# First attention: values and sums in four bursts a step instead of six

## The chip, the cores and the metric

The kernel runs on one core of one Trainium2 chip. The metric is the device time in microseconds of one execution of the whole program. Times are in microseconds (us). The engines are named PE (TensorE, matmuls), PEld (its weight loads, which overlap), DVE (VectorE), ACT (ScalarE), POOL (GpSimd) and SP (SyncE, which issues most DMAs).

## What is computed

Two transformer layers over x of 2 x 1024 x 512. The change lies in the attention of the first one, which is multi-head attention with latent keys and values, rotary parts and a causal mask:

```python
q = _rmsnorm(x @ wq_a.T, q_a_ln_w) @ wq_b.T              # 32 heads of 64 + 64 (rotary)
ckv, k_pe = ckv_kpe[..., :KVR], ckv_kpe[..., KVR:]       # latent of 32, rotary key of 64
kv = _rmsnorm(ckv, kv_a_ln_w) @ wkv_b.T                  # keys 64 and values 128 a head
scores = jnp.einsum('bqhd,bkhd->bhqk', q_full, k_full) * softmax_scale
scores = jnp.where(causal[None, None], scores, jnp.finfo(scores.dtype).min)
attn = jax.nn.softmax(scores, axis=-1)
out = jnp.einsum('bhqk,bkhd->bqhd', attn, v).reshape(B, S, H * VD)
return out @ wo.T
```

Layer norms with modulation, a feed-forward part with routed low-rank experts, a second attention with shared keys and a second feed-forward part surround it.

## The kernel before

`attention0` handles 4 heads of one batch in a **step** t; there are STEPS0 = 16 steps. Scores are computed transposed, keys on the partitions and 512 queries along the row. A step has 12 **quads** n, one for each pair of a query half qc and a key tile kt of 128 that the causal mask leaves: quads 0 to 3 are the first half (kt 0 to 3), quads 4 to 11 the second (kt 0 to 7). On the diagonal (quads 0 to 3 and 8 to 11) a quad covers 512, 384, 256 and 128 queries; the last two of these pack two and four heads in one score unit, so the quads have 4, 4, 2, 1, 4, 4, 4, 4, 4, 4, 2, 1 units, 38 a step.

For each unit PE makes three matmuls into one of two PSUM banks (`score`, L985 to L989, with a fourth, L987, for the mask on the diagonal), and ACT writes the exponential (`exps`, L886) into one of 16 slots of `at_prob`. Unit x waits until the exponential of unit x - 2 is done, and a slot until the quad that used it has been consumed (`pv_done`). Between the units PE issues **pieces**: query projections of step t + 2 (`project_q`, L1037) and matmuls for row maxima (`maximum`, L1000), which DVE reduces (L916, L921); these use a ring of 4 banks. `quad_work` lists the pieces of a quad.

`values(g, part)` (L1022) takes the probabilities of a quad through 32-column matmuls, for each of the 4 heads into its own 32 partitions: part 0 with the latents `l_cn` into the bank `at_op`, part 1 with ones into `at_dp`. In the trace each of these matmuls is two records, so two quads are x16. For quads 4 to 7 part 1 is left out: POOL adds their probabilities beforehand (`presum` 1, 2, 3, L816), and PE sums the result in `early_sums` (L1031). Before the change a burst of two quads, 10-11, 0-1, 2-3, 4-5, 6-7 and 8-9, stands behind the scores of each odd quad 1, 3, 5, 7, 9 and 11; MID_AT says how many maxima stand between its two parts.

The order of the other engines is fixed too, each in its own program. ACT: the exponentials of a quad; behind quad 2 the copy out of the second query half of the step before, behind quad 6 that of the first half (`copy_out`, L856 and L857), for which `values` of quads 0 and 4 wait (`u_copied`); behind quads 7 and 10 the conversion of a half of the projected queries of step t + 2 (`queries_hi`, L873), which waits for POOL's rotation (`rot_done`). POOL in steps 1 to 13: presum 1, rotate half 0 (L791, L792), low parts of half 0 (L802, waits for `queries_hi`), presums 2 and 3, `normalise` (L820), rotate half 1, low parts of half 1. PE turns the maxima of the step's second half with a transpose (`turn_maxima`, L1009) ahead of quad 2 (in the first step ahead of quad 4); it waits for DVE's last maximum and its join (L926). The result goes through ACT (L863) and a DMA into the queries that quad 4 needs.

Of the kernel before, what the change touches and what calls it, by code (L numbers as in the profile page):

```python
# [600 lines left out]
QUADS = UNITS // G  # L601
STEPS0 = B * NG
# [5 lines left out]
FIRST_HALF = 4 * G  # L608
OWN_AT = [{0: 8, 1: 8, 2: 8, 3: 8}, {0: 3, 1: 3}]
MAX_AT = [{6: 8, 7: 8, 8: 7, 9: 7, 10: 6, 11: 6}, {2: 4, 3: 4, 4: 5, 5: 5, 6: 4, 7: 6, 8: 4, 9: 4, 10: 3, 11: 3}]  # L610
MID_AT = {3: 2, 5: 3, 7: 3, 9: 2, 11: 2}
PROJ_AT = [{7: (0,), 8: (1, 2), 9: (3,), 10: (4, 5)}, {4: (0,), 5: (1,), 6: (2,), 7: (3,), 8: (4,), 9: (5,)}]
PROJ_FIRST = {1: (0, 1, 2), 2: (3, 4, 5)}
TURN_A, TURN_B = 9, (4, 2)
# [11 lines left out]
EARLY = [n for n, (qc, kt) in enumerate(QK) if kt < 4 * qc]  # L626
# [44 lines left out]
def attention0(nc, k, s, opened, o_dram, sums, recips, next_loads):  # L671

    with ExitStack() as ctx:
# [46 lines left out]
        with nc.Block() as block:  # L720
# [247 lines left out]
            def _(pe):  # L968
# [58 lines left out]
                def early_sums(t):  # L1027
                    pe.wait_ge(s["pre_done"], 3 * G * (t + 1))
                    pe.wait_ge(s["u_copied"], 2 * (2 * t + 1))
                    for j in range(G):  # L1030
                        mm = nc.tensor.matmul(dp[LAT * j:LAT * (j + 1), :], k.ones[:], pre[:, j, :], start=True, stop=False)  # L1031
                    mm.then_inc(s["pre_used"], 1)

                def project_q(t, u):
                    hf, part = u // 3, u % 3
                    freed(pe, "queries", t, u)
                    nc.tensor.matmul(bank("queries", t, u)[:], k.wq[:, t % NG, part, :], k.qa_t[:, t // NG, HALF * hf:HALF * (hf + 1)],  # L1037
                                     start=True, stop=True).then_inc(s["pj_ready"], 1)
# [7 lines left out]
                for g in range(STEPS0 * QUADS):  # L1046
                    t, n = divmod(g, QUADS)
                    for which in turns(t, n):
                        turn_maxima(*which)
                    if n == 0:  # L1050
                        moved(pe, lo_in, t)
                        pe.wait_ge(m_in[t % 2], 16 * (t // 2 + 1))
                    if n == 4:
                        pe.wait_ge(m_late[t % 2], 16 * (t // 2 + 1))
                    pieces = quad_work(t, n)
                    between = max(len(pieces) - MID_AT.get(n, 0), 0)
                    cut = [round(between * i / UNITS_OF[n]) for i in range(UNITS_OF[n] + 1)]
                    for i in range(UNITS_OF[n]):
                        score(t, n, i)
                        for kind, to, u in pieces[cut[i]:cut[i + 1]]:  # L1060
                            if kind == "queries":
                                project_q(to, u)
                            if kind == "max":
                                maximum(to, u)
                    if g % 2 and g >= 3:
                        for part in range(2):
                            for kind, to, u in pieces[between:] if part == 1 else ():
                                maximum(to, u)
                            if part == 1 and (g - 3) % QUADS in EARLY:
                                if (g - 2) % QUADS == EARLY[-1]:  # L1070
                                    early_sums((g - 3) // QUADS)
                                continue
                            values(g - 3, part)
                            values(g - 2, part)
                for part in range(2):
                    values(STEPS0 * QUADS - 2, part)
                    values(STEPS0 * QUADS - 1, part)


RG = 64  # L1080
# [1089 lines left out]
```

## Time and profile before

| | |
|---|---|
| median of 3 runs | 2156.2 us (2155.67 to 2158.36) |
| the profiled execution | 2149.3 us |
| its span, first to last instruction | 2147.5 us |
| PE busy | 1968.2 us (92%) |
| DVE, ACT, POOL busy | 1174.7, 903.5, 524.4 us |
| mean granted TensorE clock | 0.945 |

The first attention runs from about 145 us to 1117 us of the span. Matmuls are pipelined and their ends are modelled, so in the timeline the distance from one start to the next says more than a duration.

### The profile page before, as it was taken

The numbers are of one execution on the slowest core, as the hardware profiler recorded it, in microseconds if no ns is written. First come the engines' busy times: TensorE is split into PE (matmuls) and PEld (weight loads), VectorE is DVE, ScalarE is ACT, GpSimd is POOL, SyncE is SP. The second block draws the span as 40 slices with busy tenths as digits, with TensorE's granted clock in tenths as the row PEclk, the third lists the DMA queues.
The fourth block names the chain that finished last, engine by engine and source line by source line (L and its number), as shares of the span: only waits on it lengthen the run. The fifth ranks groups of instructions, "written<-read, shape, count | busy, mean of one in ns | idle before, by whom it ended". The sixth has DMA issues, their size and how long they took to land. (4 is left out here: it accounts for less than half of the span.)

```text
span 2147.5 us, 34578 instructions
## 1 busy us (share of the span) xinstructions
PE 1968.2 (92%) x12776; PEld 1173.9 (55%) x12776; DVE 1174.7 (55%) x2557; ACT 903.5 (42%) x1909; POOL 524.4 (24%) x408
## 2 busy tenths in 40 slices
PE   5859999999999999999977899997999999999698
PEld 4535666666666666666643454554444444444277
DVE  3546655555555555555402455446676776675078
ACT  3413344444444444444430122221666656666344
POOL 0014235555434443555330000000000000000143
PEclk9869999999999999999998999995999999999599
DMA  9752233222233323322235221144132132220121
GB/s 310 258 155 60 61 80 81 70 58 57 69 81 80 80 71 80 80 67 59 56 107 189 66 67 48 58 113 125 22 53 47 33 53 45 35 38 18 33 87 59
DMA packets 113594, 172.21 MB, mean 80 GB/s; under 512 B 26186, under 2 KB 46826, under 8 KB 113298
## 3 DMA queue, kind: packets, MB, share of 16 engines
q1 hardware_dynamic: 112402, 169.75, 29.9%
q8 instruction: 101, 1.65, 0.3%
q14 instruction: 67, 0.55, 0.1%
q10 hardware_dynamic: 1024, 0.26, 0.1%
HBM read 84.32 MB, written 29.38 MB: 53 GB/s over the span
## 5 line engine op out<-in xcount | busy, mean ns | idle before, releaser
L886 ACT ACTIVATE at_prob<-at_scp 128x512 f32<-128x512 f32 (+1 forms) x608 | 349.7, 576 | 512.2 <-PE at_scp L989 511.0
L1659 ACT ACTIVATE as_prob<-as_scp 128x512 f32<-128x512 f32 (+2 forms) x640 | 309.0, 563 | 200.3 <-PE as_scp L1769 148.9
L921 DVE CUSTOM_DVE_ANT_0 at_junk<-at_mxp,causal 128x128 f32<-128x128 f32 (+3 forms) x512 | 243.4, 488 | 188.6 <-PE at_mxp L1000 183.9
L1709 DVE TENSOR_REDUCE as_mxd<-as_mxp 128x2 f32<-128x256 f32 (+3 forms) x256 | 202.6, 820 | 98.3 <-PE as_mxp L1788 96.1
L916 DVE TENSOR_REDUCE at_mxf<-at_mxp 128x1 f32<-128x512 f32 x256 | 175.9, 687 | 141.3 <-PE at_mxp L1000 137.4
L1694 POOL TENSOR_TENSOR l_att_t<-l_att_t,as_spread 64x1024 f32<-64x1024 f32 x16 | 37.9, 2367 | 863.2 <-DMA as_spread<-l_recips 863.2
L1707 DVE TENSOR_REDUCE as_mxf<-as_mxp 128x2 f32<-128x1024 f32 x128 | 151.0, 1221 | 52.8 <-PE as_mxp L1783 52.6
L816 POOL TENSOR_TENSOR at_pre<-at_prob 128x512 f32<-128x512 f32 x64 | 80.1, 1281 | 407.2 <-ACT at_prob L886 407.2
L816 POOL TENSOR_TENSOR at_pre<-at_pre,at_prob 128x512 f32<-128x512 f32 x128 | 160.3, 1282 | 3.6 <-ACT at_prob L886 1.2
L1807 PE MATMUL as_op<-as_prob,l_vn 128*32 128x512 f32 (+3 forms) x1536 | 160.4, 540 | 0.0
L1022 PE MATMUL at_op<-at_prob,l_cn 128*32 128x512 f32 (+3 forms) x1536 | 143.7, 491 | 4.0 <-ACT at_u_sb L857 4.0
L985 PE MATMUL at_scp<-hd_early_q,l_khi 97*128 97x512 f32 (+1 forms) x304 | 137.2, 451 | 10.8 <-DMA hd_late_q<-at_slo 8.3
L985 PE MATMUL at_scp<-at_qhi,l_khi 97*128 97x512 f32 (+1 forms) x304 | 138.8, 456 | 0.8 <-ACT at_prob L886 0.5
L1000 PE MATMUL at_mxp<-l_khi,hd_early_q 96*128 96x512 f32 (+2 forms) x384 | 125.2, 379 | 10.9 <-DMA hd_early_q<-at_shi 9.3
L1000 PE MATMUL at_mxp<-l_khi,at_qhi 96*128 96x512 f32 (+2 forms) x384 | 122.5, 367 | 0.5 <-DVE at_mxf L916 0.2
L988 PE MATMUL at_scp<-hd_late_q,l_khi 96*128 96x512 f32 (+1 forms) x304 | 117.2, 386 | 0.0
L989 PE MATMUL at_scp<-hd_early_q,l_klo 96*128 96x512 f32 (+1 forms) x304 | 116.8, 384 | 0.0
L988 PE MATMUL at_scp<-at_qlo,l_khi 96*128 96x512 f32 (+1 forms) x304 | 116.8, 384 | 0.0
L989 PE MATMUL at_scp<-at_qhi,l_klo 96*128 96x512 f32 (+1 forms) x304 | 116.3, 383 | 0.0
L1766 PE MATMUL as_scp<-as_q,l_keys 49*128 49x512 f32 (+2 forms) x320 | 108.1, 463 | 7.8 <-ACT as_prob L1659 6.5
L1783 PE MATMUL as_mxp<-l_keys,hd_early_q 48*128 48x512 f32 (+2 forms) x384 | 97.7, 488 | 19.2 <-DVE as_mxf L1707 7.3
L1766 PE MATMUL as_scp<-hd_early_q,l_keys 49*128 49x512 f32 (+2 forms) x320 | 103.7, 446 | 5.7 <-ACT as_prob L1659 4.3
(248 smaller groups left out, 3480.5 us busy)
## 6 DMA issues: line engine op xcount, KB each, us to landing
hd_late_q<-at_slo SPq DMA_DIRECT2D x96, 128.0 KB, 2.4
at_qhi<-at_shi SPq DMA_DIRECT2D x96, 128.0 KB, 2.4
at_qlo<-at_slo SPq DMA_DIRECT2D x96, 128.0 KB, 2.5
hd_early_q<-at_shi SPq DMA_DIRECT2D x84, 128.0 KB, 2.5
at_spread<-l_recips SPq DMA_DIRECT2D x64, 128.0 KB, 2.7
l_o<-at_u_sb SPq DMA_DIRECT2D x16, 512.0 KB, 3.3
hd_early<-in_wmod SPq DMA_DIRECT2D x7, 1024.0 KB, 7.4
hd_late<-l_o SPq DMA_DIRECT2D x12, 512.0 KB, 4.1
```

The source lines that it names most:

```text
L816: nc.gpsimd.tensor_tensor(pre[:, j, :], other, prob[:, (x + j) % RING0, :], ALU.add).then_inc(s["pre_done"], 1)
L886: nc.scalar.activation(prob[:, x % RING0, c0:HALF], scp[x % BANKS0][:, c0:HALF], ACT.Exp).then_inc(s["exp_done"], 1)
L916: nc.vector.reduce_max(mxf[:, j, qt - 4:qt - 3], tile[:], AX_X).then_inc(s["mx_done"], 1)
L921: nc.vector.tensor_tensor_reduce(out=junk[:, u % 2, 0:w], in0=tile[:, 0:w], in1=k.causal[:, HALF - w:HALF], scale=1.0, scalar=LOWEST, op0= ...
L985: nc.tensor.matmul(out, k.khi[0:KR + 1, b, ks], q_cols(qhi[t % 2][0:KR + 1]), start=True, stop=False)
L988: nc.tensor.matmul(out, k.khi[0:KR, b, ks], q_cols(qlo[t % 2][0:KR]), start=False, stop=False)
L989: nc.tensor.matmul(out, k.klo[0:KR, b, ks], q_cols(qhi[t % 2][0:KR]), start=False, stop=True).then_inc(s["sc_ready"], 1)
L1000: nc.tensor.matmul(bank("max", t, u)[:, 0:w], qhi[t % 2][0:KR, qt // 4, j, qt % 4 * P:(qt % 4 + 1) * P], k.khi[0:KR, t // NG, k0:k0 + w], ...
L1659: nc.scalar.activation(prob[:, x % RING1, cols], scp[x % BANKS1][:, cols], ACT.Exp).then_inc(s["exp_done"], 1)
L1709: nc.vector.reduce_max(mxd[:, t % 2, :, i, qt:qt + 1], tile[:, :, 0:(qt % 4 + 1) * P], AX_X).then_inc(s["mx_done"], 1)
L1766: mm = nc.tensor.matmul(out, k.keys[rows, t // NG, kt * P:(kt + 1) * P], queries, start=True, stop=not diagonal)
L1807: mm = nc.tensor.matmul(op[2 * HD * j:2 * HD * (j + 1), c0:HALF], k.vn[:, t // NG, kt, :], prob[:, (x + j % UNITS1_OF[n]) % RING1, p0:p0 + ...
```

## The change

The values and sums are issued in bursts listed by the new table BURSTS0: behind the scores of quad 0 those of quads 8 to 11 of the step before, behind quad 4 those of quads 0 to 3, behind quad 6 the values of 4 and 5, behind quad 8 those of 6 and 7. In a burst all values come first, then the maxima that MID_AT keeps (3, 3 and 2 at quads 0, 4 and 8), then the sums; the early sums stand with the sums of quads 8 to 11. The other engines' programs are as they were. In the changed kernel the line numbers from 612 on are 1 higher (L985 is L986, L1022 is L1023, L1031 is L1032), and behind the new function `sums` 12 higher (L1037 is L1049).

```diff
--- before.py
+++ after.py
@@ -608,7 +608,8 @@
 FIRST_HALF = 4 * G
 OWN_AT = [{0: 8, 1: 8, 2: 8, 3: 8}, {0: 3, 1: 3}]
 MAX_AT = [{6: 8, 7: 8, 8: 7, 9: 7, 10: 6, 11: 6}, {2: 4, 3: 4, 4: 5, 5: 5, 6: 4, 7: 6, 8: 4, 9: 4, 10: 3, 11: 3}]
-MID_AT = {3: 2, 5: 3, 7: 3, 9: 2, 11: 2}
+MID_AT = {0: 3, 4: 3, 8: 2}
+BURSTS0 = {0: (-4, -3, -2, -1), 4: (0, 1, 2, 3), 6: (4, 5), 8: (6, 7)}
 PROJ_AT = [{7: (0,), 8: (1, 2), 9: (3,), 10: (4, 5)}, {4: (0,), 5: (1,), 6: (2,), 7: (3,), 8: (4,), 9: (5,)}]
 PROJ_FIRST = {1: (0, 1, 2), 2: (3, 4, 5)}
 TURN_A, TURN_B = 9, (4, 2)
@@ -1031,6 +1032,17 @@
                         mm = nc.tensor.matmul(dp[LAT * j:LAT * (j + 1), :], k.ones[:], pre[:, j, :], start=True, stop=False)
                     mm.then_inc(s["pre_used"], 1)
 
+                def sums(burst, between):
+                    for q in burst:
+                        values(q, 0)
+                    for kind, to, u in between:
+                        maximum(to, u)
+                    for q in burst:
+                        if q % QUADS == EARLY[-1] + 1:
+                            early_sums(q // QUADS)
+                        if q % QUADS not in EARLY:
+                            values(q, 1)
+
                 def project_q(t, u):
                     hf, part = u // 3, u % 3
                     freed(pe, "queries", t, u)
@@ -1053,7 +1065,8 @@
                     if n == 4:
                         pe.wait_ge(m_late[t % 2], 16 * (t // 2 + 1))
                     pieces = quad_work(t, n)
-                    between = max(len(pieces) - MID_AT.get(n, 0), 0)
+                    burst = [QUADS * t + i for i in BURSTS0.get(n, ()) if QUADS * t + i >= 0]
+                    between = max(len(pieces) - MID_AT.get(n, 0), 0) if burst else len(pieces)
                     cut = [round(between * i / UNITS_OF[n]) for i in range(UNITS_OF[n] + 1)]
                     for i in range(UNITS_OF[n]):
                         score(t, n, i)
@@ -1062,19 +1075,8 @@
                                 project_q(to, u)
                             if kind == "max":
                                 maximum(to, u)
-                    if g % 2 and g >= 3:
-                        for part in range(2):
-                            for kind, to, u in pieces[between:] if part == 1 else ():
-                                maximum(to, u)
-                            if part == 1 and (g - 3) % QUADS in EARLY:
-                                if (g - 2) % QUADS == EARLY[-1]:
-                                    early_sums((g - 3) // QUADS)
-                                continue
-                            values(g - 3, part)
-                            values(g - 2, part)
-                for part in range(2):
-                    values(STEPS0 * QUADS - 2, part)
-                    values(STEPS0 * QUADS - 1, part)
+                    sums(burst, pieces[between:])
+                sums(range(STEPS0 * QUADS - 4, STEPS0 * QUADS), ())
 
 
 RG = 64
```

PE at the end of a step, from the one unit of quad 11 on to the first unit of the next step. Before:

```order
L985 MATMUL at_scp<-hd_early_q,l_khi 128x512
L987 MATMUL at_scp<-after_r,ident_r 128x512
L988 MATMUL at_scp<-hd_late_q,l_khi 128x512
L989 MATMUL at_scp<-hd_early_q,l_klo 128x512
L1000 MATMUL at_mxp<-l_khi,at_qhi 128x512
L1022 MATMUL at_op<-at_prob,l_cn 32x512 x4
L1022 MATMUL at_op<-at_prob,l_cn 32x384 x4
L1000 MATMUL at_mxp<-l_khi,at_qhi 128x512
L1000 MATMUL at_mxp<-l_khi,at_qhi 128x256
L1022 MATMUL at_dp<-at_prob,ones 32x512 x4
L1022 MATMUL at_dp<-at_prob,ones 32x384 x4
L985 MATMUL at_scp<-at_qhi,l_khi 128x512
```

Now, from the same unit on:

```order
L986 MATMUL at_scp<-hd_early_q,l_khi 128x512
L988 MATMUL at_scp<-after_r,ident_r 128x512
L989 MATMUL at_scp<-hd_late_q,l_khi 128x512
L990 MATMUL at_scp<-hd_early_q,l_klo 128x512
L1001 MATMUL at_mxp<-l_khi,at_qhi 128x512 x2
L1001 MATMUL at_mxp<-l_khi,at_qhi 128x256
L986 MATMUL at_scp<-at_qhi,l_khi 128x512
L988 MATMUL at_scp<-after_r,ident_r 128x256
L989 MATMUL at_scp<-at_qlo,l_khi 128x512
L990 MATMUL at_scp<-at_qhi,l_klo 128x512
L986 MATMUL at_scp<-at_qhi,l_khi 128x512
L988 MATMUL at_scp<-after_r,ident_r 128x256
```

The values (`at_op`) and sums (`at_dp`) of quads 8 and 9 are no longer between the two steps; two units of the next step stand behind each other.

PE at the end of quad 6 (its last unit, and the first of quad 7). Before:

```order
L985 MATMUL at_scp<-hd_early_q,l_khi 128x512
L988 MATMUL at_scp<-hd_late_q,l_khi 128x512
L989 MATMUL at_scp<-hd_early_q,l_klo 128x512
L1000 MATMUL at_mxp<-l_khi,at_qhi 128x384
L985 MATMUL at_scp<-hd_early_q,l_khi 128x512
L988 MATMUL at_scp<-hd_late_q,l_khi 128x512
L989 MATMUL at_scp<-hd_early_q,l_klo 128x512
L1037 MATMUL at_mxp<-l_qa_t,l_wq 128x512
```

Now:

```order
L986 MATMUL at_scp<-hd_early_q,l_khi 128x512
L989 MATMUL at_scp<-hd_late_q,l_khi 128x512
L990 MATMUL at_scp<-hd_early_q,l_klo 128x512
L1001 MATMUL at_mxp<-l_khi,at_qhi 128x384
L1023 MATMUL at_op<-at_prob,l_cn 32x512 x8
L986 MATMUL at_scp<-hd_early_q,l_khi 128x512
L989 MATMUL at_scp<-hd_late_q,l_khi 128x512
L990 MATMUL at_scp<-hd_early_q,l_klo 128x512
```

The values of quads 4 and 5 now stand directly behind the last unit of quad 6.

PE at the end of quad 1 with the turn ahead of quad 2. Before:

```order
L989 MATMUL at_scp<-at_qhi,l_klo 128x384
L1000 MATMUL at_mxp<-l_khi,at_qhi 128x512
L1022 MATMUL at_op<-at_prob,l_cn 32x256 x4
L1022 MATMUL at_op<-at_prob,l_cn 32x128 x4
L1022 MATMUL at_dp<-at_prob,ones 32x256 x4
L1022 MATMUL at_dp<-at_prob,ones 32x128 x4
L1009 MATMUL at_mxp<-ident,at_mxd 16x128
L985 MATMUL at_scp<-at_qhi,l_khi 128x512
```

Now:

```order
L990 MATMUL at_scp<-at_qhi,l_klo 128x384
L1001 MATMUL at_mxp<-l_khi,at_qhi 128x512
L1010 MATMUL at_mxp<-ident,at_mxd 16x128
L986 MATMUL at_scp<-at_qhi,l_khi 128x512
L988 MATMUL at_scp<-after_r,ident_r 128x2x128
```

The burst of quads 10 and 11 no longer stands between the last maximum and the transpose.

## Rows read from the trace of the kernel before

**Rows 1.** Busy time by stretch; columns as in the first line.
```profile
core 0: us, PE busy (x) PEld busy (x) DVE busy (x) ACT busy (x) POOL busy (x), PEclk, DMA share, GB/s
600.00:620.00 20.00, 19.76 (x137) 12.68 (x138) 10.38 (x38) 8.85 (x17) 0.00 (x0) 1.00 0.53 130
620.00:640.00 20.00, 20.00 (x119) 13.45 (x111) 14.19 (x35) 9.64 (x19) 14.76 (x12) 1.00 0.11 29
```

**Rows 2.** Waits of PE and of ACT, 200 to 1100 us; total, times, longest.
```profile
PE at_dp L1031 <- POOL at_pre L816: 5.9, 13, 0.5
PE at_op L1022 <- ACT at_u_sb L857: 4.0, 15, 0.7
...
ACT at_shi L873 <- POOL at_tm L792: 10.3, 13, 0.8
```

**Rows 3.** Timeline of PE, quad 7's last unit and burst; start, duration.
```profile
630.01 0.40 PE L985 MATMUL at_scp<-at_qhi,l_khi 97*128 97x512 f32 x1
...
630.71 0.40 PE L1000 MATMUL at_mxp<-l_khi,hd_early_q 96*128 96x512 f32 x1
631.04 1.92 PE L1022 MATMUL at_op<-at_prob,l_cn 128*32 128x512 f32 x16
632.89 0.74 PE L1000 MATMUL at_mxp<-l_khi,hd_early_q 96*128 96x256 f32 x3
```

**Rows 4.** Timeline of PE, the early sums behind quad 9.
```profile
645.45 1.07 PE L1031 MATMUL at_dp<-at_pre,ones 128*32 128x512 f32 x8 [0.47 <-POOL at_pre L816]
646.45 0.50 PE L985 MATMUL at_scp<-at_qhi,l_khi 97*128 97x512 f32 x1
```

**Rows 5.** Timelines of PE and of DVE at the turn ahead of quad 2.
```profile
601.30 0.39 PE L1000 MATMUL at_mxp<-l_khi,at_qhi 96*128 96x512 f32 x1
601.62 0.86 PE L1022 MATMUL at_op<-at_prob,l_cn 128*32 128x256 f32 x16
...
603.06 0.28 PE L1009 MATMUL at_mxp<-ident,at_mxd 128*16 128x128 f32 x1
...
601.91 0.69 DVE L921 CUSTOM_DVE_ANT_0 at_junk<-at_mxp,causal 128x512 f32<-128x512 f32 x1 [1.04 <-PE at_mxp L1000]
...
602.64 0.17 DVE L926 TENSOR_TENSOR at_mxd<-at_mxd,at_mxf 128x16 f32<-128x16 f32 x1
```

**Rows 6.** Timelines of PE and of ACT at the two copies.
```profile
607.03 1.71 PE L1022 MATMUL at_op<-at_prob,l_cn 128*32 128x512 f32 x16 [0.24 <-ACT at_u_sb L857]
...
626.60 0.39 PE L985 MATMUL at_scp<-at_qhi,l_khi 97*128 97x512 f32 x1
...
606.28 0.60 ACT L857 ACTIVATE at_u_sb<-at_op 128x512 f32<-128x512 f32 x1
...
627.66 0.60 ACT L857 ACTIVATE at_u_sb<-at_op 128x512 f32<-128x512 f32 x1
```

**Rows 7.** Timelines of POOL, ACT and PE from quad 7 to the next step.
```profile
632.74 2.52 POOL L802 TENSOR_TENSOR at_slo<-at_tm,at_shi 128x512 fp32r<-128x512 f32 x2 [4.83 <-ACT at_shi L873]
635.22 10.17 POOL L816 TENSOR_TENSOR at_pre<-at_pre,at_prob 128x512 f32<-128x512 f32 x8
645.36 2.38 POOL L820 TENSOR_TENSOR at_u_sb<-at_u_sb,at_spread 128x1024 f32<-128x1024 f32 x1
647.71 1.29 POOL L791 TENSOR_TENSOR at_tm<-at_tm 128x512 f32<-128x512 f32 x1
648.97 1.28 POOL L792 TENSOR_TENSOR at_tm<-at_tm 128x512 f32<-128x512 f32 x1
...
630.97 0.60 ACT L886 ACTIVATE at_prob<-at_scp 128x512 f32<-128x512 f32 x1 [0.34 <-PE at_scp L989]
...
650.28 1.15 ACT L873 ACTIVATE at_shi<-at_tm 128x512 fp32r<-128x512 f32 x2 [0.82 <-POOL at_tm L792]
651.34 0.58 ACT L886 ACTIVATE at_prob<-at_scp 128x512 f32<-128x512 f32 x1
...
655.05 0.39 PE L985 MATMUL at_scp<-hd_early_q,l_khi 97*128 97x512 f32 x1
```

**Rows 8.** Busy time by stretch in the opening; columns as in rows 1.
```profile
103.40:106.00 2.60, 0.20 (x2) 0.00 (x0) 2.50 (x10) 0.60 (x1) 0.00 (x0) 1.00 1.01 353
...
108.00:109.00 1.00, 1.00 (x2) 0.50 (x2) 0.59 (x2) 0.00 (x0) 0.00 (x0) 0.50 1.11 326
```

## The prediction

> **What bounds the kernel now.** I read the busy times in stretches of 20 us first: inside the first attention TensorE (PE) is busy 19.76 and 20.00 us of 20 at a granted clock of 1.00, which is its upper level, 2.4 GHz [rows 1]. So time there is PE time: whatever is taken from PE shortens a step, whatever makes PE wait lengthens it. Next the waits by engine [rows 2]: in 900 us PE waits for another engine only in two regular places, 5.9 us in 13 times for POOL's pre-sums (0.45 us each) and 4.0 us in 15 times for ACT's copy of the output bank (0.27 us each). The third row is the one that matters most below: ACT waits 10.3 us in 13 times (0.79 us each) for POOL's rotated queries, and nothing comes of it, because PE does not need ACT at that moment. Then the timeline of one step, at the places where bursts are taken away or put in.
>
> **Part 1: fewer blocks of 32-column matmuls.** A block is a run of values, sums or early sums between full-width matmuls. The 16 instructions of 512 columns at 631.04 are followed 1.85 us later [rows 3]; the 8 at 645.45 by a score 1.00 us later [rows 4]. The difference, 0.85 us, is the work of 8, so a block has 0.15 us that doesn't grow with it. The maximum before the first of them starts at 630.71 and would be followed after 0.23 us, but the block starts at 631.04: 0.10 us on entering; on leaving I take the same 0.10. A block costs 0.35 us beside its work. Before there are 10 blocks in a step (quads 10-11 as one; two each for 0-1, 2-3, 8-9; one for 4-5; two for 6-7 with the early sums), after it 6 (two for 8-11 with the early sums, two for 0-3, one each for 4-5 and 6-7). Gain: 4 x 0.35 = 1.4 us a step.
> The Trainium skill weighs this less: TensorEngine Tiling (Array Packing), Key Properties, says that a change of tiling mode drains TensorE, and TensorE: Matmul & The Clock Gate, "What happens when you issue a matmul", puts a drain at about 128 cycles, 0.05 us at 2.4 GHz. Two changes a block would by that estimate be 0.1 us, the gain 0.4 us a step, and the end 16 us later than the sum below. The rows measure the block whole, so I stay with 0.35.
>
> **Part 2: waits that go.** The values of quad 0 now come after the scores of quad 4, so the copy at quad 2 is long done: 0.27 us gained. The early sums go from quad 9 to the next step's quad 0: POOL's pre-sums are then done, 0.45 us gained. Maxima put between scores of quads 5 and 9 instead of inside a block save about 0.1 us, but the three taken from quad 0 leave four scores in a row with nothing between, where each waits for the exponential two before it: 0.15 us lost. Together with part 1: 2.1 us gained a step.
>
> **Part 3: the turn at quad 2 loses its cover.** The transpose of the maxima (L1009) waits for DVE's last maximum of the step and its join. Its last matmul starts at 601.30; DVE works from 601.91 to 602.81; the burst of quads 10-11 filled the time until 603.06 [rows 5]. After the change nothing stands between: PE would be ready at 601.53 and gets the join at about 602.98. Loss 1.45 us, and the scores of quad 2 queue behind it. Bounds: 1.3 us (join seen at once) to 1.55 us.
>
> **Part 4: the output bank at quad 6.** Values of quad 4 start a new accumulation in the bank that ACT copies out after the exponentials of quad 6. They move from behind quad 7 to right behind quad 6. PE ends quad 6 at 626.60, or 626.70 with the entry of a block; ACT's second copy starts at 627.66 and takes 0.60 us; in another place PE started 0.15 us after such a copy ended (606.28 + 0.60 to 607.03) [rows 6]. So PE starts at 628.41: 1.7 us lost a step, all of PE's queue behind it. Bounds 1.5 to 1.9.
> Parts 1 to 4 leave 3.3 - 2.1 = 1.2 us a step lost, about 18 us in 15 steps; in the first step, where DVE is late, the burst at quad 3 covered a wait and moves behind it, some 4 us. **Local sum: +22 us.**
>
> **Part 5: POOL's chain at the end of a step.** This is the large one. POOL runs in program order: low parts of one query half (they wait for ACT's conversion behind the exponentials of quad 7), pre-sums 2 and 3, normalise, rotate the other half. In the rows: 632.74, 635.22, 645.36, 647.71, 648.97, end 650.25 [rows 7]. It can't start before ACT's last exponential of quad 7, which starts at 630.97, so its end hangs 18.7 us behind that one's end at 631.57. ACT, also in order, has the conversion of that second half between the exponentials of quads 10 and 11: 650.28, and only at 651.34 the exponential of quad 11, which ends at 651.92 [rows 7]. PE's second score of the next step needs its bank. Today PE comes there at 655.05, 3.0 us later [rows 7]: that is the cover.
> Now the time that PE takes from the last score unit of quad 7 (starts 630.01 [rows 3]) to that second score, 25.04 us, shrinks. Out of it go: the block of quads 4-5, 2 x 0.85 + 0.35 = 2.05 us; two of the maxima of quad 7, which now stand before the unit, 0.35 us; the early sums with their wait, 0.85 + 0.35 + 0.45 = 1.65 us; the values and the sums of quads 8-9, each 8 instructions of 512 columns (0.85 us), 8 of 384 (0.64 us) and a block's 0.35 us, together 3.7 us; the maximum between the first two scores of quad 0, 0.23 us. What is left is 17.1 us. POOL's chain isn't any shorter: exponential of quad 11 ends 21.9 us behind the start of that unit, plus 0.15 us for PE to see it, 22.05. **PE waits 5.0 us** at the second score of a step, behind it in its queue all else; SP's loads of the next queries wait for the same conversion, and keep their distance to their use. It holds for steps 1 to 13, those with queries to project and this chain, as the 13 waits of ACT today [rows 2]: 13 x 5.0 = 65 us. Bounds of one wait: 4.0 us if I have missed a microsecond of work in between, 5.5 us.
>
> **Part 6: the clock.** No row of the first attention's steady state shows PE at less than full clock. Nearest rows: before 106 PE stood idle for 2.4 of 2.6 us, and at 108 the granted clock is 0.50, that is 1.2 GHz [rows 8]. After 5 us of standing I expect a stretch at the lower level. How long isn't known; from nothing (it falls into the wait itself) to some 2.5 us lost each. I take 1.5: 13 x 1.5 = 20 us.
>
> **Sum.** 22 + 65 + 20 = 107 us on the profiled execution, 2149.3 + 107 = 2256. The median of the runs is 6.9 us above the profiled execution, so **2263 us** as a median.
>
> **Rivals.**
> (A) The forecast, all three terms: 2263, from 2240 to 2285. Chance 0.58.
> (B) The chain binds, the clock stays up: 2156 + 22 + 65 = 2243; with waits of 4.0 us and local losses of 0.6 us, 2156 + 10 + 52 = 2218. For it: only PE waits of several us lower the clock, and part of the lower stretch falls into the wait. Chance 0.17.
> (C) The clock also falls after the waits of 1.45 and 1.7 us in parts 3 and 4: 32 places at up to 1.7 us, 2263 + 54 = 2317. The steady state has few gaps elsewhere, which speaks against it. Chance 0.08.
> (D) POOL's chain doesn't bind, because its early part moves up with PE or because ACT isn't waited for: local losses alone, 2156 + 22 = 2178. Against it: today POOL waits 4.83 us for ACT before the chain starts [rows 7], so nothing of it can move up. Chance 0.09.
> (E) Faster: the block savings remain and the waits don't come. Its place is quad 6 and quad 2, its price is 2.1 us x 16 = 34 us, 2122. It decides if PE's time in front of the two waits is longer by 1.5 us than its instructions show, as it would be if DVE and ACT finished ahead. The rows 5 and 6 show both in the middle of their work when PE is ready. Chance 0.05.
> (F) Gains and losses cancel: POOL's chain not binding and one of parts 3 and 4 half as dear: within 0.2% of before. Chance 0.03.
> That the change does not do what it says is excluded: the instruction order shows four bursts.
>
> **How the numbers follow.** Likeliest is A, so 2263. Range: A whole and B whole, with part of C, 2216 to 2300; out are D, E, F and most of C, 0.2. A measurement can tell about 0.2% here. Slower by more than 0.2% is A to D, 0.92; within 0.2% 0.03; faster 0.05.
>
> **What the profile of the changed kernel would show.** PE waiting for ACT's exponential at a score (L985's successor) 13 times, about 5 us each; ACT waiting for POOL's rotation 13 times, about 4.9 us (today's 0.8 and the 4.05 us that part 5 takes out ahead of it); PE waiting for ACT's output copy 16 times at 1.7 us, and for DVE's join 15 times at 1.4; the waits for the pre-sums gone. Granted clock below 1.00 in the stretch behind each start of a step from 260 us on. POOL's own chain as long as before, 18.7 us from the last exponential of quad 7. Wrong would be: a step of 61 us (then D), or PE's waits at the right places but the clock at 1.00 (B).

## The result, and the profile after

The changed kernel takes 2279.6 us (median of 4 runs, 2275.6 to 2280.1), the kernel before 2157.0 us: ratio 1.0566, 95% interval 1.0549 to 1.0582. The forecast was 2263 in a range of 2216 to 2300. The profiled execution has a span of 2278.3 us against 2147.5: 130.8 us more.

The lines below are numbered differently by a few: the score L985 is now L986, the maximum L1000 is L1001, the turn L1009 is L1010, values and sums L1022 are L1023, ACT's exponential L886 is L887, its conversion of queries L873 is L874.

The busy times and the granted clock in 40 slices, from the page of the changed kernel:

```profile
PE 1998.5 (88%) x12776; PEld 1208.8 (53%) x12776; DVE 1164.0 (51%) x2557; ACT 904.2 (40%) x1909; POOL 523.7 (23%) x408
PEclk8868999999999999999999799999699999999689
```

The same 12776 matmuls; PE is busy 30 us longer (1968.2 before) and idle for the other 100. The waits from 200 to 1230 us (total, times, longest), which answer to [rows 2]:

```profile
PE at_scp L986 <- ACT at_prob L887: 61.9, 14, 4.7
PE at_op L1023 <- ACT at_u_sb L858: 26.2, 16, 1.8
PE at_mxp L1010 <- DVE at_mxd L927: 17.7, 15, 1.2
...
ACT at_shi L874 <- POOL at_tm L793: 63.3, 13, 4.9
```

PE's wait for POOL's pre-sums is gone, ACT's wait for POOL's rotated queries has grown from 10.3 to 63.3 us in the same 13 places, and PE now waits for ACT behind it. In one stretch of a step (its bounds, its length, then busy time of PE, PEld, DVE, ACT and POOL, granted clock, DMA share, GB/s), for [rows 1]:

```profile
640.00:660.00 20.00, 15.28 (x74) 11.21 (x74) 9.97 (x25) 6.96 (x14) 16.95 (x13) 0.88 0.13 30
```

**The start of a step.** PE's timeline (start, duration, line and operation, in brackets the idle time before it and what ended it), for PE's row of [rows 7]:

```profile
651.19 0.39 PE L990 MATMUL at_scp<-at_qhi,l_klo 96*128 96x512 f32 x1
656.31 0.80 PE L986 MATMUL at_scp<-at_qhi,l_khi 97*128 97x512 f32 x1 [4.72 <-ACT at_prob L887]
...
657.11 0.63 PE L989 MATMUL at_scp<-at_qlo,l_khi 96*128 96x512 f32 x1
```

A matmul of 512 columns that took 0.39 us before the wait takes 0.63 behind it. POOL in the same step:

```profile
637.13 2.53 POOL L803 TENSOR_TENSOR at_slo<-at_tm,at_shi 128x512 fp32r<-128x512 f32 x2 [6.67 <-ACT at_shi L874]
639.61 10.20 POOL L817 TENSOR_TENSOR at_pre<-at_pre,at_prob 128x512 f32<-128x512 f32 x8
649.77 2.37 POOL L821 TENSOR_TENSOR at_u_sb<-at_u_sb,at_spread 128x1024 f32<-128x1024 f32 x1
...
653.34 1.25 POOL L793 TENSOR_TENSOR at_tm<-at_tm 128x512 f32<-128x512 f32 x1
```

And ACT, from the last exponential of quad 7 to the one that PE waits for:

```profile
635.35 0.60 ACT L887 ACTIVATE at_prob<-at_scp 128x512 f32<-128x512 f32 x1 [0.21 <-PE at_scp L990]
...
654.62 1.15 ACT L874 ACTIVATE at_shi<-at_tm 128x512 fp32r<-128x512 f32 x2 [4.60 <-POOL at_tm L793]
655.68 1.06 ACT L887 ACTIVATE at_prob<-at_scp 128x512 f32<-128x512 f32 x2
```

The last exponential of quad 7 ends at 635.95, POOL's rotation at 654.6: 18.6 us. The conversion starts at once, the exponential of quad 11 a microsecond later, and PE when that is through. One stretch behind it, in the columns of the window above:

```profile
656.30:661.90 5.60, 5.59 (x16) 3.65 (x20) 0.00 (x0) 2.23 (x4) 2.11 (x2) 0.50 0.77 174
```

The clock is at 1.2 GHz in the 5.6 us behind the wait, in which PE isn't idle: 2.8 us lost. From 662 on it is back at 1.00.

**The two smaller waits**, at quad 6 and at the turn of quad 2, for [rows 6] and [rows 5]:

```profile
628.66 1.92 PE L1023 MATMUL at_op<-at_prob,l_cn 128*32 128x512 f32 x16 [1.64 <-ACT at_u_sb L858]
...
670.80 0.40 PE L1001 MATMUL at_mxp<-l_khi,at_qhi 96*128 96x512 f32 x1
...
672.15 0.18 DVE L927 TENSOR_TENSOR at_mxd<-at_mxd,at_mxf 128x16 f32<-128x16 f32 x1
672.39 0.28 PE L1010 MATMUL at_mxp<-ident,at_mxd 128*16 128x128 f32 x1 [1.19 <-DVE at_mxd L927]
```

The number in brackets counts from the modelled end of the matmul before, the prediction counted from start to start. In its way of counting the transpose is 672.39 - 670.80 - 0.23 = 1.36 us late. The burst at quad 6 follows a maximum that starts at 626.68; with 0.17 us for that one and 0.10 for the entry of a block it is 1.71 us late. The score at the start of a step is 656.31 - 651.19 - 0.23 = 4.89 us late.

**Where the 130.8 us are.** The turn at quad 9 is a mark in every step. It starts like this before (first, seventh, eighth and fifteenth step):

```profile
216.37 0.27 PE L1009 MATMUL at_mxp<-ident,at_mxd 128*16 128x128 f32 x1
578.79 0.27 PE L1009 MATMUL at_mxp<-ident,at_mxd 128*16 128x128 f32 x1
638.46 0.27 PE L1009 MATMUL at_mxp<-ident,at_mxd 128*16 128x128 f32 x1
1052.41 0.27 PE L1009 MATMUL at_mxp<-ident,at_mxd 128*16 128x128 f32 x1
```

and after:

```profile
229.96 0.27 PE L1010 MATMUL at_mxp<-ident,at_mxd 128*16 128x128 f32 x1
574.27 0.27 PE L1010 MATMUL at_mxp<-ident,at_mxd 128*16 128x128 f32 x1
642.52 0.27 PE L1010 MATMUL at_mxp<-ident,at_mxd 128*16 128x128 f32 x1
1184.24 0.27 PE L1010 MATMUL at_mxp<-ident,at_mxd 128*16 128x128 f32 x1
```

(574.27 is the mark of the sixth step, 642.52 that of the seventh.) A step in the middle takes 68.25 us instead of 59.67: +8.6, twelve times. The first mark is 13.6 us late. The second step's is another 7.0 us late (70.98 us for 64.02), the fifteenth's another 8.0 (63.86 for 55.90), and behind it 1.0 comes back: 13.6 + 7.0 + 12 x 8.6 + 8.0 - 1.0 = 130.8.

Not all of the 13.6 belongs to the change. One maximum in the opening, ahead of every moved burst, is late already. Before, then after:

```profile
177.13 0.50 PE L1000 MATMUL at_mxp<-l_khi,hd_early_q 96*128 96x512 f32 x1 [0.63 <-DVE at_pre L946]
```

```profile
181.05 0.50 PE L1001 MATMUL at_mxp<-l_khi,hd_early_q 96*128 96x512 f32 x1 [0.63 <-DVE at_pre L947]
```

These 3.9 us are mostly scatter of the opening. In the profiles of the kernels below that share before's opening that row starts from 177.1 to 180.8, in those with the changed kernel's from 179.3 to 183.8; before's is the earliest of all, in an execution that was 6.9 us faster than its median. Some 2 us between the two groups' means may belong to the change. Between this row and the first mark lie 39.2 us before and 48.9 after, 9.7 more, but that isn't the change's alone either. The kernel of experiment 9 (early_only) has the program of before up to this mark, and takes 43.2 us:

```profile
180.19 0.50 PE L1000 MATMUL at_mxp<-l_khi,hd_early_q 96*128 96x512 f32 x1 [0.63 <-DVE at_pre L946]
...
223.36 0.27 PE L1009 MATMUL at_mxp<-ident,at_mxd 128*16 128x128 f32 x1
```

Its granted clock is at 0.50 in two stretches there (from 198 to 202, for one), where the profile of before stays at 1.00. The five profiled kernels that have the changed kernel's program up to the mark take 46.8 to 50.5 us. So the change costs between 4 and 11 us in this stretch, about 7 by the means.

### The profile page after: what moved, and what is told of

Read it like the earlier page. It is cut to its first block and busy times, and to the rows that moved or that the text cites. A ratio compares the mean times of both kernels' runs of the same rounds, so it can differ in the third digit from the quotient of the medians.

```text
span 2278.3 us, 34578 instructions
## 1 busy us (share of the span) xinstructions
PE 1998.5 (88%) x12776; PEld 1208.8 (53%) x12776; DVE 1164.0 (51%) x2557; ACT 904.2 (40%) x1909; POOL 523.7 (23%) x408
## 5 line engine op out<-in xcount | busy, mean ns | idle before, releaser
L887 ACT ACTIVATE at_prob<-at_scp 128x512 f32<-128x512 f32 (+1 forms) x608 | 348.1, 575 | 557.3 <-PE at_scp L990 556.1
L986 PE MATMUL at_scp<-hd_early_q,l_khi 97*128 97x512 f32 (+1 forms) x304 | 140.7, 463 | 44.0 <-ACT at_prob L887 33.1
L986 PE MATMUL at_scp<-at_qhi,l_khi 97*128 97x512 f32 (+1 forms) x304 | 139.8, 460 | 29.1 <-ACT at_prob L887 28.8
L1023 PE MATMUL at_op<-at_prob,l_cn 128*32 128x512 f32 (+3 forms) x1536 | 142.2, 503 | 26.2 <-ACT at_u_sb L858 26.2
L1001 PE MATMUL at_mxp<-l_khi,hd_early_q 96*128 96x512 f32 (+2 forms) x384 | 124.3, 390 | 10.2 <-DMA hd_early_q<-at_shi 9.0
L989 PE MATMUL at_scp<-hd_late_q,l_khi 96*128 96x512 f32 (+1 forms) x304 | 124.0, 408 | 0.0
L990 PE MATMUL at_scp<-hd_early_q,l_klo 96*128 96x512 f32 (+1 forms) x304 | 123.4, 406 | 0.0
L1001 PE MATMUL at_mxp<-l_khi,at_qhi 96*128 96x512 f32 (+2 forms) x384 | 121.1, 377 | 2.4 <-DVE at_tm L947 2.2
L989 PE MATMUL at_scp<-at_qlo,l_khi 96*128 96x512 f32 (+1 forms) x304 | 121.4, 399 | 0.0
L990 PE MATMUL at_scp<-at_qhi,l_klo 96*128 96x512 f32 (+1 forms) x304 | 121.0, 398 | 0.0
L988 PE MATMUL at_scp<-after_r,ident_r 128*128 128x256 f32 (+1 forms) x352 | 109.5, 311 | 0.0
```

What stands on the lines that cost most here:

```text
L887: nc.scalar.activation(prob[:, x % RING0, c0:HALF], scp[x % BANKS0][:, c0:HALF], ACT.Exp).then_inc(s["exp_done"], 1)
L986: nc.tensor.matmul(out, k.khi[0:KR + 1, b, ks], q_cols(qhi[t % 2][0:KR + 1]), start=True, stop=False)
L989: nc.tensor.matmul(out, k.khi[0:KR, b, ks], q_cols(qlo[t % 2][0:KR]), start=False, stop=False)
L990: nc.tensor.matmul(out, k.klo[0:KR, b, ks], q_cols(qhi[t % 2][0:KR]), start=False, stop=True).then_inc(s["sc_ready"], 1)
L1001: nc.tensor.matmul(bank("max", t, u)[:, 0:w], qhi[t % 2][0:KR, qt // 4, j, qt % 4 * P:(qt % 4 + 1) * P], k.khi[0:KR, t // NG, k0:k0 + w], ...
```

## Experiments

Each ratio is to the kernel before, run beside it on the same chip. "Step" is the distance of two marks in the middle of the attention.

**1. The conversion leaves the chain (hi_late).** The changed kernel, ACT's conversion of the second query half moved behind the next step's exponentials of quad 0.

```diff
                         exps(t, n)
+                        if n == 0 and t >= 1 and t + 1 < STEPS0:
+                            queries_hi(t + 1, 1)
                         for which in queries_ready(t, n):
-                            queries_hi(*which)
+                            if which[1] == 0 or which[0] == 1:
+                                queries_hi(*which)
```

> The changed kernel with one move on ACT: the conversion of the second query half stands behind the exponentials of the next step's quad 0 instead of between those of quads 10 and 11. Theory (POOL's chain holds up the exponential of quad 11, and the clock falls behind that wait): PE's 62 us of waiting for exponentials go, the granted clock stays at 1.00, a step goes from 68.3 to about 60.8 us, the whole from 2279.6 to about 2183 us. Rival (the clock falls because of the long bursts or the waits at quads 2 and 6): the waits go, but the low clock stays, about 2215 us. Rival (the chain is a bystander): over 2250 us.

2191.3 us, ratio 1.0157 (1.0140 to 1.0173): 88 of the change's 123 us are gone with this one edit. PE's waits from 200 to 1230 us:

```profile
PE at_op L1026 <- ACT at_u_sb L858: 26.2, 16, 1.8
PE at_mxp L1013 <- DVE at_mxd L930: 17.8, 15, 1.2
...
PE at_scp L989 <- ACT at_prob L887: 0.3, 1, 0.3
```

The two small waits stand as they were, the 61.9 us are 0.3. The shortest steps take 60.93 us: the change without its chain costs 1.25 us a step (the forecast had 1.2). Other steps take up to 62.86. In one of these the clock falls behind the wait at quad 6, and the 16 values take 3.50 us instead of 1.92:

```profile
655.58 3.50 PE L1026 MATMUL at_op<-at_prob,l_cn 128*32 128x512 f32 x16 [1.64 <-ACT at_u_sb L858]
```

Over 60.93 the twelve middle steps have 5.7 us together, most of the 8 between expectation and result. What the full step of the changed kernel has on top, 68.25 - 60.93 = 7.3 us, is the wait of 4.7 and 2.6 for the clock (4.9 and 2.4 if the wait is counted from start to start).

**2. A shorter chain (norm_late).** The changed kernel, POOL rotates before it normalises, which takes 2.4 us out of the chain.

```diff
+                    if t + 2 < STEPS0:
+                        rotate(t + 2, 1)
                     if t >= 1:
                         normalise(t - 1)
                     if t + 2 < STEPS0:
-                        rotate(t + 2, 1)
                         low_parts(t + 2, 1)
```

> The changed kernel with POOL's rotation of the second query half ahead of the normalise step, so that the chain is shorter by the 2.4 us of normalise. Theory: PE's wait at the second score of a step falls from 4.7 to about 2.4 us, 13 x 2.4 = 31 us less. If the clock falls only behind a wait of several us, another 13 x 2.4 us go with it, 2217 us in all; if it falls as long as before, 2248 us. If the chain isn't the cause, no change (2279.6 us).

2239.8 us, 1.0395 (1.0370 to 1.0421), between the two expectations. The wait is shorter by about what left the chain, and the stretch at the lower clock by half: 3.4 us instead of 6.8 in most steps. PE's timeline, then the window behind it:

```profile
639.22 0.49 PE L987 MATMUL at_scp<-at_qhi,l_khi 97*128 97x512 f32 x1 [2.45 <-ACT at_prob L888]
...
639.67 0.39 PE L990 MATMUL at_scp<-at_qlo,l_khi 96*128 96x512 f32 x1
```

```profile
640.50:643.90 3.40, 3.40 (x16) 1.72 (x18) 0.00 (x0) 1.71 (x3) 1.79 (x2) 0.50 0.89 200
```

After 2.45 us of standing PE works 1.3 us at 2.4 GHz and then 3.4 us at 1.2. Most steps take 64.97 us; 60.93 + 2.45 (the wait) + 3.4/2 is 65.08. I had expected either no stretch or the whole one.

**3. The copy (copy_early).** The changed kernel, the copy of the output bank behind the exponentials of quad 5 (`if n == 6:` becomes `if n == 5:` before `copy_out(t, 0)`).

> The changed kernel with ACT's copy of the first query half's output behind the exponentials of quad 5 instead of quad 6. Theory: PE's 26.2 us of waiting for that copy go (16 x 1.64 us), and since this place lies ahead of POOL's chain nothing takes them back: 2253 us. Rival (the chain's wait grows by what is saved): no change, 2279.6 us.

2255.0 us, 1.0456 (1.0439 to 1.0473). The wait at quad 6 is no longer in the list, the one at the start of a step is untouched:

```profile
PE at_scp L986 <- ACT at_prob L887: 63.1, 16, 4.8
```

26.2 us of waits gone, 24.5 us of time: a wait on PE's path counts nearly in full. It doesn't feed the chain either, because POOL's chain hangs on quad 7, which comes later and moves along.

**4. The price of a block (no_mid).** The kernel before with `MID_AT = {}`: the maxima stay with the scores, and four blocks of 32-column matmuls in a step are no longer cut in two.

> The kernel before with no maxima kept inside the bursts (MID_AT empty): they stand between the scores, and values and sums of a burst are one block. 10 blocks of 32-column matmuls a step become 6 with all other places as they were; behind quad 7 the number of blocks stays 1. Theory (a block costs 0.35 us beside its work, as taken in the prediction): 16 x 4 x 0.35 = 22 us less, 2135 us. By the drain of the Trainium skill (0.1 us a block): 6 us less, 2151 us. If DVE then makes PE wait, less than that.

2141.0 us, 0.9931 (0.9916 to 0.9946). The step is 58.65, 1.03 us shorter. PE's waits:

```profile
PE at_dp L1031 <- POOL at_pre L816: 13.5, 13, 1.1
PE at_op L1022 <- ACT at_u_sb L857: 0.6, 1, 0.6
```

The wait for the pre-sums has grown from 0.45 to 1.04 us, since PE is there sooner and POOL is not; the copy's 0.27 has gone. Four blocks are therefore worth 1.03 + 0.59 - 0.27 = 1.35 us, 0.34 each. The 6 us missing against the 2135 expected are mostly this longer wait, 13 x 0.59 = 8 us.

**5. Quads 8 and 9 apart (split89).** The changed kernel, with the values of quads 8-9 and the early sums behind quad 11, and only 10-11 in the next step's quad 0.

```diff
-BURSTS0 = {0: (-4, -3, -2, -1), 4: (0, 1, 2, 3), 6: (4, 5), 8: (6, 7)}
+BURSTS0 = {0: (-2, -1), 4: (0, 1, 2, 3), 6: (4, 5), 8: (6, 7), 11: (8, 9)}
```

> The changed kernel with the burst of quads 8 to 11 taken apart again: quads 8 and 9 with the early sums behind quad 11, quads 10 and 11 behind the next quad 0 (5 bursts). This undoes one part of the change. Theory: 3.7 us of values and sums and 1.2 us of early sums stand again in front of the second score of a step, so PE's wait of 4.7 us there goes and with it the low clock; one block more costs 0.35 us. A step of 68.3 becomes about 61.3 us, the whole 2279.6 - 13 x 7.0 = 2189 us. Rival (the chain hangs on the early sums' place in some other way, or the clock on the long burst of quads 0 to 3): over 2230 us.

2212.3 us, 1.0258 (1.0243 to 1.0273). PE and ACT (from each engine's waits):

```profile
PE at_scp L986 <- ACT at_prob L887: 8.4, 14, 0.6
...
ACT at_shi L874 <- POOL at_tm L793: 64.1, 13, 5.0
```

ACT waits for POOL as long as in the changed kernel, and PE hardly notices: the burst is the cover. ACT's own wait is no sign of harm. The miss of 23 us: the quicker steps take 62.1 us and not 61.3, since 0.6 us of PE's wait is left; five of the middle steps take 63.7 to 64 us, with 3.4 us at the lower clock behind the wait at quad 6; and the second step is 2.5 us longer than in the changed kernel.

**6. The first step (first3).** The changed kernel, its burst of quads 0-3 behind quad 3 in the first step only (with three maxima kept inside it).

> The changed kernel, in the first step alone the burst of quads 0 to 3 stands behind quad 3 instead of quad 4, and so in front of the turn as before the change. Theory: the first step's loss (the start of its quad 9 went from 216.4 to 230.0 us, 13.6 us) is PE's uncovered wait for DVE's last maximum and the low clock that follows it: 8 to 10 us less, 2270 us. Rival (it is the second burst order itself): no change, 2279.6 us.

2275.2 us, 1.0552 (1.0534 to 1.0569), 4 us below the changed kernel; the intervals overlap, so the time alone doesn't settle it. The mark of the first step does, 4.8 us earlier than the changed kernel's 229.96:

```profile
225.20 0.27 PE L1011 MATMUL at_mxp<-ident,at_mxd 128*16 128x128 f32 x1
```

The burst covers the turn again, and the clock is low for a shorter stretch. The 4.8 us are about half of the 8 to 10 expected. Both kernels still pay the copy's wait there.

**7. The turn (own42).** The changed kernel, maxima of quads 0 and 1 divided 4 and 2 instead of 3 and 3 (`OWN_AT = [..., {0: 4, 1: 2}]`), so that DVE has less left at the turn.

> The changed kernel with the step's own maxima as 4 and 2 on quads 0 and 1 instead of 3 and 3, so that the last one stands ahead of quad 1's last unit. Theory: PE's wait at the turn, 1.18 us a step, is covered by a unit of 0.65 us: 15 x 0.65 = 10 us less, 2270 us. With the chain's wait in the same step untouched nothing takes it back. Rival (the wait moves to the exponentials of quad 1): no change.

2281.3 us, 1.0572 (1.0556 to 1.0588): the same as the changed kernel. The wait is shorter, from 17.7 to 7.8 us, and yet nothing is gained. PE's timeline at quad 6 and the window of that burst show why:

```profile
492.36 3.62 PE L1023 MATMUL at_op<-at_prob,l_cn 128*32 128x512 f32 x16 [1.64 <-ACT at_u_sb L858]
```

```profile
492.40:495.80 3.40, 3.40 (x16) 0.67 (x16) 0.00 (x0) 0.00 (x0) 1.75 (x2) 0.51 0.18 48
```

The wait of 1.64 us is the one that the changed kernel has in each step without harm. Here five steps, every other one from 352 to 902 us, have 3.4 us at 1.2 GHz behind it, 1.7 us lost in each, which takes back most of the 10 us that the turn gives. So it is rival C's mechanism, in a kernel for which I hadn't named it. Why it strikes here and not there is open.

**8. All four repairs (all4).** The changed kernel with the edits of hi_late, copy_early, own42 and first3 together.

> The changed kernel with four moves at once: the second conversion behind the next quad 0, the copy behind quad 5, own maxima 4 and 2, the first step's burst behind quad 3. Theory: the four bursts then keep their gain without the waits: a step of 60.9 (conversion moved) less 1.64 (copy) less 0.65 (turn) is 58.6 us against 59.7 before, the whole 2156 - 15 x 1.1 = 2140 us. Rival (the savings of the bursts are smaller than taken): 2156 or more.

2165.1 us, 1.0039 (1.0024 to 1.0053). The best steps take 59.24, others 59.8 to 61.7. PE has new waits, for loads that follow the late conversion:

```profile
PE at_mxp L1005 <- DMA at_qhi<-at_shi: 5.6, 7, 1.6
PE at_mxp L1005 <- DMA hd_early_q<-at_shi: 5.3, 7, 1.7
```

Moving the conversion back opens the one wait and exposes the next thing in line: SP's loads of the queries. The three slowest middle steps (61.7 to 61.9 us) are the ones where such a wait lasts 1.4 to 1.6 us and 3.4 us at 1.2 GHz follow (at 321, 741 and 802 us); in the other slower steps the granted clock stays at 1.00. The result is 25 us above what I expected.

**9. Only the early sums (early_only).** The kernel before, early sums with the sums of quads 8-9 behind quad 11.

> The kernel before with another part of the change alone: the early sums stand with the sums of quads 8 and 9, behind quad 11, instead of behind quad 9. Theory: PE's wait for POOL's pre-sums (0.45 us a step) and one block (0.35 us) go, 13 to 16 x 0.8 us less: 2144 us. The 0.8 us leave the cover of POOL's chain, which stays above zero. Rival (the wait returns at the new place, or the block isn't a cost): no change, 2157 us.

2144.7 us, 0.9943 (0.9930 to 0.9955), step 58.83 (-0.85). The wait for the pre-sums is gone, 0.45, and there is one block less, so a block is worth 0.40 here.

**10. Both (early_nomid).** early_only with `MID_AT = {}`.

> The kernel before with the early sums behind quad 11 and no maxima inside bursts: 6 blocks a step, and no waits of the new order. Theory: the 58.65 us of a step without maxima inside bursts less PE's 1.04 us of waiting for POOL there, 57.6 us, the whole 2141 - 15 = 2126 us. Rival (POOL's chain then reaches PE at the second score of a step, since its cover is down to about 1 us): 2135 to 2145 us.

2121.7 us, 0.9844 (0.9831 to 0.9858): faster than both kernels. Most steps take 57.40. The busy times of one stretch of 60 us:

```profile
560.00:620.00 60.00, 60.00 (x379) 40.73 (x379) 35.53 (x100) 27.51 (x51) 27.68 (x22) 1.00 0.31 75
```

From 58.83 to 57.40 are 1.43 us; 0.27 of it is the copy's wait. The trace of early_only has 9 blocks in a step and this one 6, so three blocks are worth 1.16 us, 0.39 each.

**11. Only quad 6 (q45).** The kernel before, with the values of quads 4 and 5 right behind quad 6.

```diff
+                    if n == 6:
+                        values(g - 2, 0)
+                        values(g - 1, 0)
```

(and none behind quad 7 in return)

> The kernel before with one part of the change alone: the values of quads 4 and 5 stand behind quad 6 instead of quad 7. Blocks, sums and everything else are as before. Theory: ACT's copy isn't done when PE comes, 16 x 1.64 us = 26 us more, 2183 us. The 2.05 us that leave the way from quad 7 to the next step use up most, not all, of the 3.0 us of cover ahead of the exponential of quad 11, so that one doesn't make PE wait; ACT's wait for POOL grows from 0.8 to about 2.9 us. Rival: a single wait of 1.6 us is enough for the lower clock, then up to 1.7 us more a step, up to 2210 us.

2218.3 us, 1.0285 (1.0270 to 1.0301), step 63.43 in most steps and 65.1 in some. This one move costs 3.75 us a step, and the time lies 35 us above the theory and above the rival's 2210 too. Its waits:

```profile
PE at_dp L1031 <- POOL at_pre L816: 19.2, 13, 1.5
PE at_mxp L1000 <- DVE at_tm L946: 5.3, 14, 0.4
```

The wait for the copy (1.64), 1.0 more for the pre-sums, since less work stands between quad 7 and the early sums than before, and 0.6 for DVE (the row shown, and 0.2 at the turn). Some 0.5 us of the step I can't assign. Three steps have 3.4 us at 1.2 GHz behind the copy's wait.

ACT's wait for POOL was to grow to 2.9 us and stays at 0.8 (10.3 us in 13 places). PE now stands longer for POOL's pre-sums ahead of the early sums, so the way from there to the exponential of quad 11 is as long as before. Where the early sums leave quad 9 (early_only), PE isn't held there, and ACT waits 32.6 us in the same 13 places, 2.5 each. By these numbers the wait of 0.45 us in the kernel before kept PE in step with POOL's chain.

**12. Single blocks, late (five).** Five bursts without cuts: quads 10-11 behind quad 1, 0-3 behind 4, 4-5 behind 7, 6-7 behind 9, 8-9 with early sums behind 11; in the first step 0-3 behind 3.

```diff
-MID_AT = {0: 3, 4: 3, 8: 2}
-BURSTS0 = {0: (-4, -3, -2, -1), 4: (0, 1, 2, 3), 6: (4, 5), 8: (6, 7)}
+MID_AT = {}
+BURSTS0 = {1: (-2, -1), 4: (0, 1, 2, 3), 7: (4, 5), 9: (6, 7), 11: (8, 9)}
+FIRST_BURSTS = {3: (0, 1, 2, 3), 7: (4, 5), 9: (6, 7), 11: (8, 9)}
```

> Five bursts a step, each one block: quads 10-11 behind quad 1 (in front of the turn, as before the change), 0 to 3 behind quad 4, 4-5 behind quad 7 and 6-7 behind quad 9 (as before), 8-9 with the early sums behind quad 11; the first step keeps quads 0 to 3 behind quad 3. It joins the one pair of bursts of the change whose joining uncovers no wait. Theory: one block less than the six of the kernel with early sums behind quad 11 and no maxima inside bursts, which took 2121.7 us: 16 x 0.35 = 6 us less, 2116 us, no new wait of PE, clock at 1.00 in the steady state. Rival (longer bursts cost something of their own, or DVE then runs late between quads 1 and 4): 2122 us or more.

2160.4 us, 1.0024 (1.0012 to 1.0035), 44 us above what I expected. PE and DVE (from each engine's waits), and PE's timeline at quad 4:

```profile
PE at_mxp L1002 <- DVE at_slo L942: 22.1, 12, 2.4
...
DVE at_shi L940 <- DMA at_qlo<-at_slo: 19.4, 6, 4.0
```

```profile
680.74 1.01 PE L1002 MATMUL at_mxp<-l_khi,at_qhi 96*128 96x512 f32 x2 [2.18 <-DVE at_slo L942]
681.68 4.49 PE L1024 MATMUL at_op<-at_prob,l_cn 128*32 128x512 f32 x32
```

Without a burst behind quad 3 PE comes to quad 4's projections sooner than DVE, whose conversion waits until the low query loads have left its buffer. The clock falls behind this wait too in 8 of the middle steps: here the 32 values take 4.49 us. It is a cover that I hadn't looked for, between two engines and a load.

## Why the prediction came out as it did

**Parts 1 and 2 (blocks, waits that go)** hold. A block measures 0.34, 0.40 and 0.39 us (experiments 4, 9 and 10) against 0.35; the waits of 0.45 and 0.27 are gone. The rule of the Trainium skill weighed there (TensorEngine Tiling (Array Packing), Key Properties, with the drain of TensorE: Matmul & The Clock Gate, 0.1 us a block by estimate) gives less than a third of what is measured. The measurement decides.

**Part 3 (turn)**: 1.36 us from start to start instead of 1.45, inside the bounds. DVE's join ends 1.53 us behind the start of the last maximum (1.51 before); PE starts 0.06 us after it, where 0.17 was taken.

**Part 4 (copy)**: 1.71 us from start to start where 1.7 was forecast, in 16 places (1.64 in PE's list of waits), shown by copy_early. The same move costs 3.75 us in the kernel before (q45): 1.0 of it is a longer wait for the pre-sums, which can't come here, where the early sums have left that place.

**Local sum of a step**: forecast 1.2, measured 1.25 in hi_late. The agreement is partly luck: 1.45 + 1.7 is 3.15 and not the 3.3 of the prediction, so its terms add up to 1.05, and as measured (1.36 and 1.71 lost, about 2.1 gained) to 0.95. Some 0.3 us elsewhere in a step was missed, which no run isolates.

**The opening is the term that was sized worst.** I put some 4 us on the first step. By the marks it is 9.7 between the two profiles, of which up to 4 are scatter (see the result). For the second step nothing was set aside, and it has 7.0 where the local 1.2 stood. The windows over both in the changed kernel (columns as above):

```profile
184.00:201.00 17.00, 11.98 (x31) 7.80 (x34) 7.03 (x19) 4.18 (x9) 7.48 (x6) 0.50 0.49 112
...
244.00:248.00 4.00, 4.00 (x12) 3.00 (x11) 2.95 (x8) 1.63 (x3) 1.14 (x2) 0.50 0.00 0
```

17 us at 1.2 GHz, with PE busy 11.98 of them: 6.0 us lost. In the profile of before the granted clock of the same stretch is 1.00. The uncovered turn adds 2.12 - 0.38 = 1.7 us, the load behind it 2.90 - 2.23 = 0.7, the copy 1.4: 9.8 together. In the second step PE waits 2.4 us for DVE around 241 (0.4 before), and 6.8 us at the lower clock follow, 3.4 lost. I treated the opening as a place with one wait more. It is where the clock falls most easily: four of the kernels that are built on before (no_mid, early_only, early_nomid, q45) have 3.4 to 10.2 us at 1.2 GHz between 182 and 204 us of the span, and each waits 2.3 to 3.3 us for a load there.

**Part 5 (the chain)** is right in mechanism, place and size. The chain measures 18.6 us (18.7 forecast), the wait 4.72, or 4.89 from start to start (5.0), ACT's wait 4.9 (4.9), thirteen times; hi_late takes the conversion out and 88 us with it, split89 puts cover back and PE's wait falls to 0.6.

**Part 6 (the clock)** has the right sign and too small a size: 1.5 us a step taken, 2.4 to 2.6 measured as a difference of steps and 2.8 from the window, at or just beyond the bound of 2.5. None of the rows that I had read of before showed how long the lower level lasts; the one that I had was next to a stretch with PE idle. 13 x 1.1 = 14 us by the larger of the two.

**Sum.** Forecast +107 on the profiled execution, measured +130.8. Of the 24 us between, 3.9 are the opening's scatter, 9.7 - 4 = 5.7 the first step (up to 4 of them scatter of before's profile again), 7.0 - 1.2 = 5.8 the second, 12 x 0.9 + 0.3 = 11 the thirteen with the chain (clock 14 more, wait 3 less), and the tail gives back 2. The profiled execution of before took 7.7 us less than the median and that of after did not, so the medians are only 122.6 apart, and the 6.9 us added for the median leave 2263 some 17 us short.

**Rivals.** B (clock stays up) and D (no chain) fall by the windows and the waits; E and F with them. C is half right: in the changed kernel the clock stays at 1.00 behind the waits at quad 6 and at the turn in the middle steps, and yet own42, split89, hi_late and q45 show it falling behind the same 1.64 us in some of their steps, and all4 behind waits of 1.4 to 1.6 us for a load. Of the signs that I named for the changed kernel, all came: 13 waits of about 5 us, ACT's 4.9, 16 copies, 15 joins, a clock below 1.00 behind each start.

What stays open is why a wait of 1.64 us lowers the clock in some steps and not in others; the 0.3 us a step that the local sum lacks; the 0.5 us a step in q45; and how much of the opening's difference is the change, since the two profiles scatter there by as much as the term.

## What to carry to other kernels

Before you move a burst, write down every chain on other engines that runs beside it with a fixed length, from the event of PE that starts it to the place where PE needs its end, and subtract the work that leaves that distance; a chain through two in-order engines (POOL, then ACT ahead of an unrelated exponential) is the one that a list of waits hides, because it shows there as an idle time that harms nobody. Merging blocks pays 0.34 to 0.40 us each and moving only what shortens a wait pays that wait: the version with just these two (early_nomid) is 1.6% faster than before, while the four large bursts with the same merging are 5.7% slower. A wait on TensorE should be priced with the slower stretch behind it: here each of the 13 waits of 2.45 us and of the 13 of 4.72 us had one, and waits of 1.4 to 1.7 us had one in some steps.

## What the runs showed of the hardware

- The granted clock stood at 1.2 GHz for 3.4 us behind waits of 1.64 us (some steps of own42, split89, hi_late and q45) and of 2.45 us (norm_late), for 6.8 us around and behind one of 4.72 us, and for 17 us in the opening. It cost half of the time that PE was busy in them. Behind most waits of 1.64 us, and behind waits of 2.2 and 2.3 us in the opening of before and no_mid, it stayed at 2.4 GHz.
- After the wait of 2.45 us PE ran another 1.3 us at 2.4 GHz (0.39 us a matmul of 512 columns) before it fell to 1.2 (0.63 us); after that of 4.72 us it started at the lower level.
- Going into and out of a block of 32-column matmuls costs 0.34 to 0.40 us in full-width work (no_mid, early_only, early_nomid).
- The opening scatters: the row at about 180 us by up to 4.5 us between kernels with the same program up to it, and the way from it to the first mark by 3.9 us between before (39.2) and early_only (43.2), in one at 2.4 GHz and in the other partly at 1.2, so differences of a few us between two profiles should be taken from marks behind it.
